# A decoder layer on one core: cross-attention heads on 64-row tiles, set-up spread over engines, new orders and banks, 71 expert blocks

## The chip, the core and the metric

The kernel runs on one core of one Trainium2 chip. Its engines are TensorE (PE in the profile, PEld its weight loads), VectorE (DVE), ScalarE (ACT), GpSimd (POOL) and SyncE (SP), each with its own queue of instructions; they wait for each other on semaphores. The metric is the time of one execution in microseconds (us), as the device measures it.

## The reference

128 sequences of 64 tokens with 128 features (8192 tokens) go through one decoder layer, all in float32:

```python
x = x + self_attention(layernorm(x))      # 16 heads of 8, rotary positions, causal softmax
x = x + xattn(layernorm(x), ctx)          # q, k, v from x and ctx; score = q k^T / dk, NO softmax;
                                          # (score v) wo + bo, residual, layer norm with gain and bias
x = x + ffn(layernorm(x))                 # 8 experts, top-1 by x @ centroids.T:
    # h = relu(xn @ w1[e].T + b1[e]); y = x + h @ w2[e].T + b2[e]; sigmoid(affinity) mixes y and x
```

As the cross-attention has no softmax, (q k^T) v is computed as q (k^T v), for each head a product of an 8x8 matrix.

## The kernel before

**Rounds.** The tokens are 64 tiles of 128, two a group, 32 groups. Each engine runs its own loop of 40 rounds (`rounds`); in round i it does each of its steps for group i minus that step's stage number (`stage(g, k, step)`), in a hand-searched order, the `one(g)` of its block. All waits are semaphore waits inside the steps. Buffers are double: `g - 2` must have been used before `g` is written.

**The way of a group.** VectorE `stats_x`, GpSimd `std_x`, ScalarE `norm_x`, TensorE `x_turned`, ScalarE `x_turned`; TensorE `queries_keys` (L560) and `values` (L568); VectorE `rotate` (L1104) and `partners` (the shuffle, L1114), GpSimd `rotated` (L1480), ScalarE `by_head` (L901). TensorE `max_scores` (L580, L588) gives scores in four banks; VectorE `row_max` (L1122, twice) reduces them, ScalarE `max_high` and GpSimd `max_low` (L1487) split the maxima in two bf16 parts, TensorE `max_rows` (L602) turns them, VectorE `max_by_head` (L1131) writes the shift. TensorE `scores` (L614, L622) writes shifted scores into the same four banks, ScalarE `exp` (L917, twice) empties them, TensorE `weighted` (L638, twice), VectorE `weighted_turned` and `inverse`, GpSimd `divide`, VectorE `turned_back`, TensorE `projected` (L655, L659), VectorE `x1_sum` (L1164, then statistics), GpSimd `std_x1`, ScalarE `norm_x1`, and so to the cross-attention: `ctx_turned`, `cross_keys_values` (L677, L681), `values_keys` (L702, k^T v on 32-column tiles of the array), VectorE `own_head` (L1174, keeps the heads' own 8x8 blocks), `cross_queries` (L689), `attended` (L717, on 32x32 tiles), `cross_output` (L723, L727), VectorE `y_sum`. Then `x2_sum`, `stats_x2`, TensorE `x2_turned` (L736) and `affinities` (L743), VectorE `choose`, TensorE `ranks`, VectorE `place` and `slots`, `alpha`, and GpSimd `scatter_rows` (L1570), two indirect DMAs that write 136 floats a token into its expert's part of `expert_rows` in DRAM. GpSimd also does `gain`, `offset_x1`, `std_y`, `std_x2`, `row_scalars` and `scaled_affinity`.

**Banks.** PSUM has eight banks; 0 to 3 are for `scores` and `max_scores`, 4 to 7 are shared by the other uses (`BANK`). `free` waits for the readers of a bank's former uses (`BEFORE`; in rounds 10 to 22 only for the first in the list).

**Set-up.** ScalarE issues four loads and then ten more (L1011, L1013). VectorE takes the mean out of the self-attention weights (L1093), then makes all masks, identities and picks (`masks_and_picks`, L1273 to L1310) after its round 0, and `bias_parts` (L1314 to L1348, biases split into three bf16 parts) after round 1. TensorE computes three constant products (L803 to L805).

**Late in the rounds.** From round 36 on, `expert_offsets` (L771) puts 16 products of single columns ahead of TensorE's round, four times. When the last counts are known, VectorE makes the block table, a chain of small operations (L1378 to L1398).

**Experts.** 72 blocks of 128 rows, each of one expert. SyncE loads a block's rows (L491), VectorE normalises (L1406), TensorE L819, L829, L840, ScalarE and VectorE the relu (L1040, L1416), GpSimd the base (L1612) and the index (L1615), VectorE the sum (L1424, L1429), GpSimd scatters 128 rows to the output (L1621).

## Time and profile before

| | us |
|---|---|
| median of the runs (lowest, highest) | 698.96 (697.45, 699.39) |
| the profiled execution | 700.01 |
| its span (first to last instruction) | 698.1 |
| TensorE busy | 595.6 (85%) |
| VectorE busy | 511.2 (73%) |
| GpSimd busy | 485.7 (70%) |
| ScalarE busy | 424.5 (61%) |

A row of a timeline gives start and length in us, engine, line and operation, what is written from what, shapes and a count; rows with the same line are merged if they follow each other. In brackets stands how long the engine was idle before it and what ended that ("remote": no event in the trace explains it; "issue": the engine waited for nothing that the profile shows). The ends of TensorE's products are modelled, so its completions are better read from who starts after them.

### The profile page before, as it was taken

Reading aid. Unit: us, or ns where it says so; the run is one execution under the profiler, and the core shown is the slowest. Engines: PE = TensorE matmul, PEld = TensorE weight load, DVE = VectorE, ACT = ScalarE, POOL = GpSimd, SP = SyncE. Lnnn points to the kernel's source line nnn. Section 1 sums busy time; section 2 is a strip of 40 time slices with the busy share of each in tenths; the row PEclk is TensorE's granted clock in tenths of the full one; section 3 lists DMA queues with packets and bytes.
Section 4 is the critical chain, followed back from the end, with each engine's and each line's share of the span. In section 5 each row is a group of like instructions: output and inputs, shape, how many; then the busy total and the mean of one; then the engine's idle time right before and its main releaser. Section 6 shows DMA issues by size and latency. Waiting matters only on the chain.

```text
span 698.1 us, 27653 instructions
## 1 busy us (share of the span) xinstructions
PE 595.6 (85%) x9104; PEld 453.4 (65%) x9136; DVE 511.2 (73%) x1813; ACT 424.5 (61%) x1154; POOL 485.7 (70%) x899
## 2 busy tenths in 40 slices
PE   3579888988888888888899888987858999999993
PEld 2246656666666566665666666655758989888893
DVE  5766887888788887888788887865455666666662
ACT  1347766767577666767677676764206666666661
POOL 2214676777767776777767776666644898898985
PEclk9999999999999999999999999999558999999997
DMA  4942111111111111111111111100022222222210
GB/s 125 168 137 85 49 38 37 34 40 49 42 33 40 49 33 41 34 40 49 37 37 41 42 40 34 33 23 18 9 61 53 60 61 62 61 64 56 65 51 5
DMA packets 53786, 35.61 MB, mean 51 GB/s; under 512 B 14464, under 2 KB 50049, under 8 KB 53648
## 3 DMA queue, kind: packets, MB, share of 16 engines
q1 hardware_dynamic: 47136, 23.29, 12.9%
q0 software_dynamic: 4352, 8.66, 3.7%
q10 hardware_dynamic: 2160, 1.87, 0.9%
q8 instruction: 79, 1.29, 0.8%
q14 instruction: 59, 0.48, 0.2%
HBM read 24.53 MB, written 9.80 MB: 49 GB/s over the span
## 4 chain that ended last, share of the span: by engine, by line
POOL 31%; DVE 22%; issue 21%; PE 18%; another core or an unknown queue 4%; POOLq 1%; DMA 1%; ACT 1%; DVEq 0%; SPq 0%; ACTq 0%
POOL bs L1612 8%; POOL qk L1480 5%; POOL pay L1542 4%; POOL rs_T L1507 3%; POOL out L1621 3%; DVE t__1 L1104 2%; PE side L659 2%; PE quad L622 2%; DVE shift L1131 2%; PE side L560 2%; DVE stat_T L1082 2%; POOL x L1516 2%; PE quad L614 2%; DVE x L1164 2%
## 5 line engine op out<-in xcount | busy, mean ns | idle before, releaser
L917 ACT ACTIVATE prob<-quad 128x1024 f32<-128x1024 f32 x64 | 65.8, 1032 | 85.9 <-remote 71.8
L1122 DVE TENSOR_REDUCE mx<-quad 128x16 f32<-128x1024 f32 x64 | 77.9, 1220 | 23.4 <-PE quad L588 23.4
L1621 POOL DMA_INDIRECT out<-yo,idi x72 | 77.9, 1081 | 21.1 <-issue 11.7
L901 ACT ACTIVATE ex<-qk,cf 128x512 f32<-128x512 f32 x128 | 81.8, 713 | 7.6 <-POOL qk L1480 7.6
L1570 POOL DMA_INDIRECT expert_rows<-pay,sli x64 | 67.4, 1053 | 21.3 <-issue 15.4
L840 PE MATMUL quad<-w,hT 128*128 x576 | 77.3, 277 | 1.0 <-DVE yb L1424 1.0
L840 PEld LDWEIGHTS quad<-w,hT 128*128 128x128 f32 x576 | 70.6, 193 | 1.8 <-issue 1.8
L1406 DVE TENSOR_SCALAR xh<-rb 128x128 f32<-128x128 f32 x72 | 47.6, 660 | 31.4 <-issue 26.5
L1612 POOL TENSOR_SCALAR bs<-rb 128x128 f32<-128x128 f32 x72 | 57.7, 802 | 10.7 <-DMA rb<-expert_rows 6.7
L1480 POOL TENSOR_TENSOR qk<-t__0 128x512 f32<-128x512 f32 x16 | 20.3, 1268 | 53.6 <-DVE t__0 L1114 48.3
L717 PE MATMUL side<-q,mt 32*32 32x64 f32 x1024 | 37.7, 225 | 19.3 <-issue 18.2
L1480 POOL TENSOR_TENSOR qk<-t__1 128x512 f32<-128x512 f32 x16 | 20.3, 1268 | 46.1 <-DVE t__1 L1114 46.1
L1051 ACT ACTIVATE w1b<-w,gb 128x512 f32 x72 | 51.7, 719 | 1.0 <-issue 1.0
L1164 DVE TENSOR_TENSOR x<-side,xr 128x256 f32<-128x256 f32 x32 | 13.6, 425 | 50.0 <-remote 33.6
L717 PEld LDWEIGHTS side<-q,mt 32*32 32x32 f32 x1024 | 24.0, 106 | 32.3 <-issue 28.6
L638 PE MATMUL side<-prob,vau 128*32 128x64 f32 x2048 | 42.4, 222 | 1.9 <-issue 0.6
L1429 DVE SCALAR_TENSOR_TENSOR yo<-yb,rb,bs 128x128 f32<-128x128 f32 x72 | 25.5, 355 | 25.2 <-DVE yb L1424 22.0
L560 PE MATMUL side<-xT,ws 128*128 128x256 f32 x128 | 38.5, 426 | 6.4 <-DVE t__0 L1104 5.9
L829 PE MATMUL quad<-xhT,w1b 128*128 128x128 f32 x288 | 41.4, 288 | 2.1 <-ACT w1b L1051 2.1
L829 PE MATMUL side<-xhT,w1b 128*128 128x128 f32 x288 | 41.3, 288 | 0.1
L1040 ACT ACTIVATE hT<-quad,b 128x128 f32<-128x128 f32 x72 | 22.6, 364 | 30.4 <-PE quad L829 22.0
L1040 ACT ACTIVATE hT<-side,b 128x128 f32<-128x128 f32 x72 | 22.5, 364 | 28.3 <-PE side L829 23.2
(195 smaller groups left out, 1708.6 us busy)
## 6 DMA issues: line engine op xcount, KB each, us to landing
rb<-expert_rows SPq DMA_DIRECT2D x72, 68.0 KB
xin<-in_x SPq DMA_DIRECT2D x32, 128.0 KB, 2.1
cin<-in_ctx SPq DMA_DIRECT2D x32, 128.0 KB, 2.2
xr<-in_x SPq DMA_DIRECT2D x32, 128.0 KB, 2.4
w<-in_w1t SPq DMA_DIRECT2D x4, 512.0 KB, 4.5
w<-in_w2t SPq DMA_DIRECT2D x4, 512.0 KB, 5.3
out<-yo,idi POOLq DMA_INDIRECT x72
expert_rows<-pay,sli POOLq DMA_INDIRECT x64
```

The costliest lines, as they stand in the source:

```text
L560: last = mm(BANK["queries_keys"][:, i * TG:(i + 1) * TG], w, xT[g.par][:, :], start=True, stop=True)
L717: last = mm(BANK["attended"][strip, own], mt2[g.par][strip, b, j, :], q2[g.par][strip, own], start=True, stop=True, tile_position=(32 * c, ...
L829: last = mm(HT[u][c // 2][:, (c % 2) * P:(c % 2 + 1) * P], w1b[u][:, c * P:(c + 1) * P], xhT[u][:, :], start=True, stop=True)
L840: last = mm(M[1][:, 0:D], hT[u][:, c, :], w2[:, bass.ds(e, 1), c, :], start=c == 0, stop=c == FC - 1)
L901: act(ex[g.par][:, i, :, :].rearrange("p a t -> p (a t)"), qk[g.par][:, :, :].rearrange("p a t -> p (a t)"), ACT.Copy, scale=own4[:, i:i + ...
L917: act(prob[g.par][:, 2 * h_:2 * h_ + 2, :], quad[:, 2 * h_:2 * h_ + 2, :], ACT.Exp).then_inc(*ac_a.done(f"e{h_}"))
L1051: act(w1b[u][:, :], w1[:, bass.ds(e, 1), :].rearrange("p e f -> p (e f)"), ACT.Copy, scale=gb[:, 0, bass.ds(e, 1)]).then_inc(*ffn["act_w1" ...
L1122: v.tensor_reduce(mx[g.par][:, 2 * h_:2 * h_ + 2, :], quad[:, 2 * h_:2 * h_ + 2, :].rearrange("p r (h k) -> p r h k", k=SQ), AX.X, ALU.max ...
L1480: v.tensor_tensor(qk[g.par][:, :, :], t1[g.par][:, :, :], t3[g.par][:, :, :], ALU.subtract).then_inc(*po_f.done("qk"))
L1570: v.indirect_dma_start(out=rows, out_offset=bass.IndirectOffsetOnAxis(ap=sli[g.par][:, j:j + 1], axis=0), in_=pay[g.par][:, j, :], in_offs ...
L1612: v.tensor_scalar(bs[q][:, :], rb[q][:, 0:D], rb[q][:, C_R:C_R + 1], rb[q][:, C_C:C_C + 1], ALU.mult, ALU.subtract).then_inc(*ffn["pool_ba ...
L1621: v.indirect_dma_start(out=o_rows, out_offset=bass.IndirectOffsetOnAxis(ap=idi[b.c % 4][:, 0:1], axis=0), in_=yo[b.c % 4][:, :], in_offset ...
```

## The change

- NBLK is 71: whatever the counts, 64 tiles in 8 experts fill at most 64 + 7 blocks.
- `values_keys` and `attended` use 64-row, 64-column tiles of the array (two strips for four); `mt2`, the mask and `own_head` are twice as wide.
- `ranks` does three products for four, with one more, zero, column group in `ohb`.
- Set-up: `masks_and_picks` and `bias_parts` are cut up. VectorE does `identities` (eight small operations) in round 0 before it centres the weights; `centred` (seven) and `picks` (twelve) behind `partners` of group 1; `key_value_bias` behind `max_by_head` of group 0 and `output_bias` behind that of group 1, eight operations each on 256 columns. ScalarE's `masks` (six copies: bvx, pick, two shifts, tri_b, negq_b) stands behind its `x_turned` of group 1; `max_scores` waits for it. TensorE's three constant products stand behind `queries_keys` of group 1, and write bank 4. GpSimd clears `pay` and `vau` behind `std_x` of group 1. The ten loads go from ScalarE's queue to SyncE's: three after round 0, seven after round 1. ScalarE issues `ws` first.
- The places of the uses in banks 4 to 7, the waits that go with them, and the orders of all five engines are new; stage numbers shift with them (TensorE's run from 1 to 7 for 0 to 6).

```diff
@@ constants of the program
-    NBLK = NT + E
+    NBLK = NT + E - 1
...
-        mt2 = two("mt2", [P, 2, J, 32])
+        mt2 = two("mt2", [P, 2, J, SQ])
...
@@ BANK (new places; scores and max_scores keep banks 0 to 3, queries_keys 7, cross_queries and values 6)
         BANK = {
+            "x2_turned": bank[4],
+            "cross_output": bank[6],
+            "x_turned": bank[7],
+            "weighted": bank[5],
+            "affinities": bank[4],
+            "x1_turned": bank[7],
+            "cross_keys_values": bank[6],
+            "max_rows": bank[4],
+            "ranks": bank[5],
+            "values_keys0": bank[4],
+            "values_keys1": bank[5],
+            "ctx_turned": bank[7],
+            "projected": bank[4],
+            "attended": bank[5],
...
-        N_CONST, N_LATE, N_WEIGHTS = 10, 4, 8
+        N_CONST, N_BIAS, N_LATE, N_WEIGHTS = 3, 7, 4, 8
         LOAD_AT = 4
+        KV_READY, OUT_READY = 8, 9
+        SETUP = bank[4]
...
             def late_loads(i):
 
+                if i == 0:
+                    for dst, src in ((cf[:, i1:cf.shape[1]], consts[:, i1:cf.shape[1]]), (nqf[:, :], negq),
+                                     (nkf[:, :], negk)):
+                        sp.dma_start(dst, src).then_inc(d_const, 16)
+                if i == 1:
+                    for dst, src in ((br[:, :, :].rearrange("p a d -> p (a d)"), brow.partition_broadcast(P)),
+                                     (wc[:, :, :], wcross), (cT[:, :], cent)):
+                        sp.dma_start(dst, src).then_inc(d_bias, 16)
+                    for q in range(4):
+                        sp.dma_start(wop[32 * q:32 * q + 32, :],
+                                     wself.rearrange("(r i d) a n -> i a r d n", r=4, i=4)[q, 5, :, :, :]
+                                     ).then_inc(d_bias, 16)
                 k = i - LOAD_AT
...
-                stage(g, 1, load_x)
-                stage(g, 3, load_ctx)
+                stage(g, 5, load_ctx)
                 stage(g, 5, load_again)
+                stage(g, 0, load_x)
...
@@ block.tensor: what a bank's use waits for (only the first of each list in the steady rounds)
+                "cross_output": [(ac_f, "V1", 3), (ac_t, "Q2", 0), (ac_t, "kv", 0), (dv_t, "y1", -1)],
+                "x1_turned": [(ac_f, "xT", 4), (ac_t, "cT", 1), (dv_f, "k2", 3), (ac_t, "xT", -1)],
+                "cross_keys_values": [(dv_t, "y1", -1), (ac_f, "V1", 2), (ac_t, "Q2", -1), (ac_t, "kv", -1)],
+                "max_rows": [(dv_r, "i1", -4), (ac_r, "xT", -4), (dv_t, "x1", -2), (dv_t, "mt", -3),
+                "values_keys0": [(dv_s, "x", 2), (dv_r, "i1", -2), (ac_r, "xT", -2), (dv_t, "x1", 0),
+                "values_keys1": [(dv_r, "tot", -2), (dv_a, "ot", 1), (ac_t, "A", -1), (dv_t, "mt", -1)],
+                "projected": [(dv_t, "mt", -1), (dv_s, "x", 1), (dv_r, "i1", -3), (ac_r, "xT", -3),
+                "attended": [(dv_t, "mt", 0), (dv_r, "tot", -2), (dv_a, "ot", 1), (ac_t, "A", -1)],
...
+            def constants():
+
+                pe.wait_ge(d_bias, 16 * N_BIAS)
+                pe.wait_ge(s_masks, 1)
+                to = SETUP
+                mm(to[:, 0:D], bvx[:, :], WO, start=True, stop=True)
+                mm(to[:, D:2 * D], mean_m[:, :], wc[:, 0, :], start=True, stop=True)
+                mm(to[:, 2 * D:2 * D + E], mean_m[:, :], cT[:, :], start=True, stop=True).then_inc(s_pe, 1)
+                setup["bank"] = to
...
-                    for c in range(4):
-                        strip = slice(32 * c, 32 * c + 32)
+                    for c in range(2):
+                        strip = slice(64 * c, 64 * c + 64)
                         for b in range(2):
                             rows_ = slice(64 * b, 64 * b + 64)
-                            last = mm(BANK[f"values_keys{b}"][strip, j * 32:(j + 1) * 32], kv2[g.par][rows_, j, 0, strip],
+                            last = mm(BANK[f"values_keys{b}"][strip, j * SQ:(j + 1) * SQ], kv2[g.par][rows_, j, 0, strip],
                                       kv2[g.par][rows_, j, 1, strip], start=True, stop=True,
-                                      tile_position=(64 * b, 32 * c))
+                                      tile_position=(64 * b, 64 * c))
...
-                        for c in range(4):
-                            strip = slice(32 * c, 32 * c + 32)
+                        for c in range(2):
+                            strip = slice(64 * c, 64 * c + 64)
                             last = mm(BANK["attended"][strip, own], mt2[g.par][strip, b, j, :], q2[g.par][strip, own],
-                                      start=True, stop=True, tile_position=(32 * c, 32 * c))
+                                      start=True, stop=True, tile_position=(64 * c, 64 * c))
                 last.then_inc(*pe_t.done("A"))
...
-                mm(bank_[:, 0:J * E], tri_b[:, :], ohb[g.par][:, :, :].rearrange("p j e -> p (j e)"),
+                mm(bank_[:, 0:(J + 1) * E], tri_b[:, :], ohb[g.par][:, :, :].rearrange("p j e -> p (j e)"),
                    start=True, stop=False)
-                for to, i in ((1, 0), (2, 0), (2, 1)):
-                    last = mm(bank_[:, to * E:(to + 1) * E], ones_b[:, :], ohb[g.par][:, i, :],
-                              start=False, stop=to == i + 1 == J)
+                mm(bank_[:, E:3 * E].rearrange("p (a e) -> p a e", e=E), ones_b[:, :],
+                   ohb[g.par][:, 0, :].unsqueeze(1).broadcast_to((P, 2, E)), start=False, stop=False)
+                last = mm(bank_[:, 2 * E:3 * E], ones_b[:, :], ohb[g.par][:, 1, :], start=False, stop=True)
...
@@ block.tensor, one round (old lines left out)
+                stage(g, 7, x2_turned)
+                stage(g, 6, cross_output)
+                stage(g, 1, x_turned)
+                stage(g, 4, weighted, 0)
+                stage(g, 7, affinities)
+                stage(g, 4, weighted, 1)
+                stage(g, 5, x1_turned)
+                stage(g, 5, cross_keys_values)
                 stage(g, 3, max_rows)
+                stage(g, 7, ranks)
                 stage(g, 1, queries_keys)
                 stage(g, 5, cross_queries)
                 stage(g, 3, scores)
+                stage(g, 5, values_keys)
+                stage(g, 3, ctx_turned)
+                stage(g, 2, values)
                 stage(g, 4, projected)
                 stage(g, 5, attended)
                 stage(g, 2, max_scores)
...
@@ block.scalar, one round (old lines left out)
+                stage(g, 8, token_ids)
                 stage(g, 4, max_high)
+                stage(g, 7, squares)
                 stage(g, 6, x1_turned)
                 stage(g, 8, exp_affinity)
+                stage(g, 6, cross_keys_values)
                 stage(g, 3, by_head)
                 stage(g, 6, cross_queries)
                 stage(g, 4, exp, 0)
+                stage(g, 4, exp, 1)
+                stage(g, 1, norm_x)
                 stage(g, 6, attended)
+                stage(g, 4, ctx_turned)
+                stage(g, 3, values)
                 stage(g, 7, x2_turned)
                 stage(g, 5, norm_x1)
                 stage(g, 1, x_turned)
...
@@ block.vector: where the pieces of set-up stand
+                    identities()
...
+                if g.n == 1:
+                    centred()
+                    picks()
...
+                if g.n == 0:
+                    key_value_bias()
+                if g.n == 1:
+                    output_bias()
...
-                                side[:, 2:2 + 2, 0:J * 32].rearrange("p b (j d) -> p b j d", d=32),
-                                headmask32[:, :].unsqueeze(1).unsqueeze(1).broadcast_to((P, 2, J, 32)), ALU.mult
+                                side[:, 0:0 + 2, 0:J * SQ].rearrange("p b (j d) -> p b j d", d=SQ),
+                                headmask64[:, :].unsqueeze(1).unsqueeze(1).broadcast_to((P, 2, J, SQ)), ALU.mult
...
@@ block.vector, one round (old lines left out)
+                stage(g, 8, x2_sum)
+                stage(g, 3, partners)
+                stage(g, 6, x1_sum)
+                stage(g, 8, stats_x2)
+                stage(g, 4, row_max, 0)
+                stage(g, 4, row_max, 1)
+                stage(g, 7, y_sum)
+                stage(g, 8, choose)
+                stage(g, 5, weighted_turned)
+                stage(g, 0, stats_x)
+                stage(g, 4, max_by_head)
                 stage(g, 5, inverse)
+                stage(g, 8, place)
+                stage(g, 2, rotate)
                 stage(g, 8, slots)
                 stage(g, 8, alpha)
                 stage(g, 5, turned_back)
+                stage(g, 6, own_head)
...
@@ block.gpsimd, one round (old lines left out)
                 stage(g, 7, std_y)
+                stage(g, 8, row_scalars)
                 stage(g, 5, divide)
                 stage(g, 1, std_x)
+                stage(g, 6, offset_x1)
                 stage(g, 8, scatter_rows)
+                stage(g, 5, std_x1)
                 stage(g, 2, rotated)
                 stage(g, 7, std_x2)
+                stage(g, 3, max_low)
+                stage(g, 7, scaled_affinity)
                 stage(g, 6, gain)
```

## Rows read from the trace of the kernel before

**Rows 1.** Windows: stretch; busy of PE, PEld, DVE, ACT, POOL; clock; DMA; GB/s.

```profile
0.00:22.00 22.00, 6.06 (x16) 3.71 (x16) 14.52 (x59) 3.62 (x8) 4.89 (x15) 1.00 0.65 127
...
145.00:431.00 286.00, 251.97 (x4880) 178.16 (x4898) 238.42 (x860) 198.81 (x540) 210.39 (x420) 1.00 0.13 40
```

**Rows 2.** Timeline of the set-up, all engines.

```profile
5.65 3.26 ACTq L1013 DMA_DIRECT2D wop<-in_wself  x4
...
7.25 0.55 DVE L1093 TENSOR_TENSOR ws<-ws,quad 128x384 f32<-128x384 f32 x1 [3.06 <-PE quad L505]
...
8.96 0.69 ACT L875 ACTIVATE xn<-xin,rs_L 128x128 f32<-128x128 f32 x2 [4.71 <-issue]
...
14.99 2.05 PE L560 MATMUL side<-xT,ws 128*128 128x256 f32 x4
...
21.59 1.66 DVE L1104 SCALAR_TENSOR_TENSOR t__0<-side,bc,cf 128x256 f32<-128x256 f32 x4
```

**Rows 3.** L614 and L1570 by source line: ns min/median/max, first and last start.

```profile
L614 PE MATMUL quad<-shift,pick x96: 379/379/634, 35.8 to 473.5; 128*128 128x512 bf16 x96
...
L1570 POOL DMA_INDIRECT expert_rows<-pay,sli x64: 957/1062/1202, 88.5 to 513.6; - x64
```

**Rows 4.** Timeline of TensorE in one even round.

```profile
302.95 1.12 PE L622 MATMUL quad<-ex,qk 32*64 32x256 f32 x32
...
304.13 0.61 PE L659 MATMUL side<-wop,ont 128*128 128x128 f32 x4
304.67 0.42 PE L717 MATMUL side<-q,mt 32*32 32x64 f32 x14
...
306.14 0.49 PE L717 MATMUL side<-q,mt 32*32 32x64 f32 x13 [0.44 <-issue]
...
309.40 0.60 PE L580 MATMUL quad<-negq_b,ii 64*128 64x512 bf16 x4
...
309.94 1.12 PE L588 MATMUL quad<-ex,qk 32*64 32x256 f32 x32
```

**Rows 5.** Timeline of GpSimd in the same round.

```profile
303.33 1.09 POOL L1570 DMA_INDIRECT expert_rows<-pay,sli  x1 [0.18 <-issue]
304.72 1.04 POOL L1570 DMA_INDIRECT expert_rows<-pay,sli  x1 [0.30 <-issue]
```

**Rows 6.** Timeline of ScalarE and VectorE in the same round.

```profile
304.32 0.61 DVE L1197 SCALAR_TENSOR_TENSOR pay<-yg,rs_U,x 128x128 f32<-128x128 f32 x2
...
306.26 1.02 ACT L917 ACTIVATE prob<-quad 128x1024 f32<-128x1024 f32 x1 [2.74 <-remote]
306.46 0.42 DVE L1164 TENSOR_TENSOR x<-side,xr 128x256 f32<-128x256 f32 x1 [1.53 <-remote]
...
307.55 0.74 DVE L1114 STREAM_SHUFFLE t__1<-t__1 128x512 f32<-128x512 f32 x1
...
308.17 0.48 DVE L1082 BATCH_NORM_STATS2 stat_R<-pay 128x6 f32<-128x128 f32 x2
```

**Rows 7.** Timelines of an early round, before the first scatter of rows.

```profile
64.25 1.02 ACT L917 ACTIVATE prob<-quad 128x1024 f32<-128x1024 f32 x1 [1.06 <-PE quad L622]
...
64.69 0.65 PE L717 MATMUL side<-q,mt 32*32 32x64 f32 x32
```

**Rows 8.** Groups by line, 145 to 431 us: busy us, mean ns | idle before, releaser.

```profile
L1174 DVE TENSOR_TENSOR mt<-side,headmask 128x128 f32<-128x128 f32 x20 | 5.6, 281 | 0.0
...
L602 PE MATMUL side<-ident_b,mt 128*32 128x64 bf16 x80 | 4.7, 194 | 17.6 <-POOL mt L1487 17.6
```

**Rows 9.** Chain of waits at the end of the rounds: start, us, what.

```profile
493.38 3.41 PE quad L771 x16
...
503.52 3.49 PE quad L771 x16
```

**Rows 10.** Timeline of GpSimd in the experts.

```profile
601.79 1.08 POOL L1621 DMA_INDIRECT out<-yo,idi  x1 [0.16 <-issue]
...
604.02 1.09 POOL L1621 DMA_INDIRECT out<-yo,idi  x1 [0.16 <-issue]
```

334 lines of the change are left out of this document (137 added, 197 removed).

## The prediction, made before the change was run

> **What bounds the kernel now.** I read the busy times by stage first, then the timeline of one round, then what its waits are. The span has three parts: a set-up, 32 groups moving through a pipeline that advances one group a round, and 72 blocks of the experts. In [rows 1] no engine is full in the rounds: from 145 to 431 us, TensorE is busy 252.0 of 286, VectorE 238.4, GpSimd 210.4, ScalarE 198.8. The first product of `scores` starts at 35.8 and the last group's at about 473 [rows 3]; with 31 steps between them that is 14.1 us a step, and the even rounds in the middle take 14.3 (286 us hold 20 of them). So a round is 14.3 us, against 11.9 of VectorE's work and 12.6 of TensorE's. The question is which loop of waits makes up the difference.
>
> The timeline of a round shows it. `scores` (L622) starts at 302.95 and its records end by 304.07; `projected` (L659) starts at 304.13 and lasts 0.61 [rows 4]. Yet ScalarE starts its exponential at 306.26 and VectorE starts `x1_sum` at 306.46, after 2.74 and 1.53 us of idling [rows 6]. In the same stretch the 32 products of `attended` (L717) come in three bursts, from 304.67 to 306.63, 1.96 us in all [rows 4]. In a round before any rows are scattered, the same 32 products take 0.65 us and the exponential starts at 64.25, right behind L622 [rows 7]. What is new in the later rounds is the pair of row scatters on GpSimd, at 303.33 and 304.72, ending at 305.76 [rows 5]. I read this as a **hold**: TensorE's completions are not reported from about 0.8 us after the first scatter's start until 0.4 us after the second one's end. That the scatter causes it is an inference from this coincidence. From `x1_sum` the loop runs on: the shuffle, then on GpSimd the rotated queries, two deviations, the gain, the offset, and only then the small sum for which `max_rows` (L602) waits, 17.6 us in 20 rounds [rows 8]; then shift, `scores`, `projected`, and again `x1_sum`.
>
> In the experts GpSimd sets the pace: a scatter starts at 601.79 and the next at 604.02, hence 2.23 us a block [rows 10].
>
> **The change part by part.**
>
> *One block fewer.* 71 for 72 takes out one beat of GpSimd, 2.2 us. The tables shrink by one column in 72: nothing.
>
> *Set-up.* Now VectorE has the centred weights at 7.80 (7.25 plus 0.55) but turns to the first `rotate` only at 21.59, with masks and bias parts in between; ScalarE issues its ten loads before its first norm at 8.96, and `queries_keys` starts at 14.99 [rows 2]. Afterwards only the small identities come first, and they lie in the wait for TensorE's mean product. ScalarE issues four loads, and SyncE ten others, seven of them queued ahead of its third load of x; the four of `wop` alone take 3.26 us to issue [rows 2], so that load goes out near 7.5 instead of at once after the first norm, and VectorE's third statistics, which stand ahead of the first `rotate`, end near 10.8. The chain is then: centred weights at 7.8, the transpose and copy of x about 0.8 more, the product 2.05 [rows 2], which ends near 10.7 as well. So `rotate` comes at about 10.8 instead of 21.59, 10.8 us earlier. What is late next: ScalarE's masks (some 3 us, ahead of the first `by_head`), TensorE's three constant products behind them, and VectorE's `centred` and `picks` ahead of the first row maxima. I let these take 1 us back. The two bias splittings (eight steps each) follow the first two shifts, where VectorE idled; if that cover were absent, each would cost about 3.3. Bounds: gain 3 (nearly all the moved work surfaces) to 12; I take 10, nearer the top, because VectorE was busy only 14.5 of the first 22 us [rows 1] and the early rounds are thin. `max_scores` waits on ScalarE's masks; behind it on TensorE stand round 3's products, which have nothing to do earlier.
>
> *Cross heads on 64-row tiles.* `values_keys` and `attended` go from 32 recorded products each to 16. The masked copy `own_head` doubles from 128x128 to 128x256: 281 ns now [rows 8]; the sum of 128x256 elements out of PSUM, `x1_sum`'s first step, takes 0.42 [rows 6]; so +0.14 us a round on VectorE. On TensorE, 32 products take 0.65 with about 0.21 for the last one alone: they follow each other by 14 ns, so halving their number saves at most 0.2, and their tiles are wider. I take 0, bounds -0.2 to +0.2. The Trainium skill ("TensorE: Matmul & The Clock Gate", section "Wait — 56ns, not 53.3ns?") says that start-to-start never drops below about 25 ns however small a product is. By that rule halving the products would save about 0.4 us in each of the two steps; the row with 14 ns speaks against it, and I leave it out.
>
> *Three rank products.* Four become three, 0.05 us at the most, off any wait: nothing.
>
> *Orders and banks.* Here lies the sum. Walk the new order with the old durations. VectorE's whole round, back to back, is 11.9 + 0.14 plus some 0.4 of small waits between dependent steps: 12.5. TensorE's floor is 14.3 less its wait at L602 (17.6/20 = 0.9) less 1.3 of hold in L717 (1.96 - 0.65): 12.1. GpSimd has 10.5 of work. A loop through both now decides: `projected` is put on the bank that `own_head` reads, and stands behind it. So per round: `own_head`'s end, a hop of 0.15, `projected` 0.65, `attended` 0.5, `max_scores` 0.55 + 1.12 + 0.15 until it is reported [rows 4], then VectorE from the row maxima to `own_head`. The last is 12.5 less what VectorE does outside the loop: `x2_sum` 0.61, shuffle 0.7, `x1_sum` 1.08 (306.46 to 307.54), the statistics of x2 0.6 (0.48 and their aggregates) [rows 6], together 3.0, so 9.5. Sum: 0.15 + 0.65 + 0.5 + 1.82 + 9.5 = 12.6, with hops **12.8 us a round without a hold**. `max_low` no longer stands behind the offset on GpSimd, and only three of its steps (two deviations, the rotation) lie ahead of it; it gets to it before the new place of `max_by_head`. The exponentials have `values_keys` to `attended`, about 2.4 us, to run beside; they need 2 x 1.02 [rows 6]. So I find no other loop over 12.6.
>
> Does the hold go? The scatter of a group now starts after `slots` and `alpha`, late in VectorE's round, with only `turned_back` and `own_head` behind them, which is while TensorE does `projected`, `attended` and `max_scores`. The first scatter's start to `projected`'s report was 303.33 to 306.3, 3.0 us [rows 5, 6]. If that stays, the loop is: `alpha`'s end, 0.15, 3.0, `x1_sum` 1.08, statistics 0.6, then the row maxima to `alpha` (9.5 less `turned_back` and `own_head`, 0.8: 8.7) = **13.5, with hops 13.6 us a round with the hold**. Bounds of this term: 12.6 to 14.3 and, if the hold adds to the first loop, above.
>
> About 27 rounds carry the full load (the first scatter at 88.5 us, the last `scores` at 473 [rows 3]). With the hold they gain 0.7 x 27 = 18.9; without, 1.5 x 27 = 40.5.
>
> *Drain.* The expert offsets (L771) stand ahead of the round on TensorE and are on the path: 3.41 and 3.49 us [rows 9], the second hiding some 2. TensorE's stages are one later, so three of the four parts come ahead of its last rank product instead of two. I count 1 us lost, bounds -2 to +4.
>
> *Sum*, against the profiled execution's 700.0 (median 699.0, so 1 less at the end): -2.2 - 10 + 1 - 18.9 = -30.1, hence 669.9 and **669 us**.
>
> **The rivals.**
> 1. *The hold goes away* (64-row tiles, half the products in flight, other neighbours). For it: no hold shows in the rounds without scatter, and none beside the experts' scatters, where TensorE works on whole tiles. Against: the scatters stay, and `max_scores` has the same 32x64 tiles as `scores`. 688.8 - 40.5 - 1 = 647.
> 2. *The order brings nothing*: another loop, or waits longer than my hops, keep 14.3; this is also the case that the search doesn't do what it says. For it: my walk counts hops of 0.15 us, and the banks are four for sixteen uses. Set-up and block alone: 688.
> 3. *Slower: the hold adds to the new loop.* The scatters now fall on `attended` and `max_scores`, whose report opens both row maxima; if max_scores is held the full 2.1 us (304.07 to 306.1) with nothing beside it, a round is 12.8 + 2.1 = 14.9, +16 us, and the total 704. It decides from the point where a round passes 14.7 (11.2 us gained elsewhere over 27 rounds is 0.41). Against: the scatter starts behind VectorE's last steps, and by then most of the wait lies beside `x2_sum` and the shuffle.
>
> **How the numbers follow.** Hold stays 0.47 (own range 660 to 680), rival 1 0.25 (640 to 656), rival 2 0.18 (682 to 692), rival 3 0.07, and 0.03 for a small net change. The range 643 to 689 leaves out the lower end of rival 1, the upper of rival 2 and rival 3. Two us (0.3%) are about what a measurement can tell from no change. Faster 0.91, same 0.02, slower 0.07.
>
> **What would show it.** Right: first `rotate` near 11 us and first `scores` near 26; steady rounds of 13.6; `x1_sum` or the first row maximum idle behind a late report while two scatters run; 71 blocks at 2.23. A round near 12.8 with the row maxima right behind L588 is rival 1; 14.3 with GpSimd or a bank wait ahead of `max_rows` is rival 2; L588's consumers 2 us late is rival 3. Wrong altogether if ScalarE's masks or the ten loads on SyncE's queue push the first rounds back, or if the drain grows by more than 4 us.

## The result, and the profile after

The changed kernel takes **682.8 us** (median, 682.6 to 683.3) against 698.6 us in the same comparison (697.5 to 699.4): a ratio of 0.978, interval 0.976 to 0.979. The forecast was 669 with a range of 643 to 689. Faster it is, but by 15.8 us and not by 30. The profiled execution took 682.6 us, with a span of 680.7, against 698.1 before, so 17.4 us of span are to be found. The ratios here and below are worked out over the single runs and are not those of two medians; they leave out one run of 896.8 us and one of 1295.9 us of the kernel before, in a slow state.

The windows answer to [rows 1]: stretch, its length, busy time of PE, PEld, DVE, ACT, POOL, clock, DMA share, GB/s.

```profile
0.00:22.00 22.00, 11.98 (x62) 6.58 (x62) 12.63 (x54) 10.15 (x23) 8.31 (x19) 1.00 0.42 109
145.00:431.00 286.00, 271.58 (x4409) 184.57 (x4436) 259.45 (x892) 214.15 (x564) 220.95 (x437) 1.00 0.14 40
```

TensorE does twice the work in the first 22 us (11.98 for 6.06), and in the rounds it goes from 252.0 to 271.6 busy us of 286. The timeline of the set-up, VectorE and then TensorE, answers to [rows 2]:

```profile
10.79 1.66 DVE L1223 SCALAR_TENSOR_TENSOR t__0<-side,bc,cf 128x256 f32<-128x256 f32 x4 [0.33 <-PE side L596]
...
25.65 0.29 PE L640 MATMUL side<-ident_b,mt 128*32 128x64 bf16 x4 [4.49 <-POOL mt L1536]
28.17 1.49 PE L653 MATMUL quad<-shift,pick 128*128 128x512 bf16 x3 [0.22 <-issue]
...
35.13 0.69 PE L686 MATMUL side<-cf,cin 128*128 128x128 f32 x2 [4.23 <-DMA cin<-in_ctx]
...
37.58 2.01 PE L626 MATMUL quad<-ex,qk 32*64 32x256 f32 x32
```

`rotate` starts at 10.79, 10.8 us earlier than before, and `max_rows` (L640) at 25.65, 7.7 earlier (before it was 33.3). Then TensorE stands 4.2 us for the first context, and the second `max_rows` comes at 42.8, where before had it at 46.7: the lead over the kernel before is down to 3.9.

One even round, from the timeline of all engines; it answers to [rows 4 to 6]:

```profile
306.13 0.61 PE L697 MATMUL side<-wop,ont 128*128 128x128 f32 x4
306.19 1.09 POOL L1619 DMA_INDIRECT expert_rows<-pay,sli  x1 [0.98 <-DVE pay L1349]
306.67 0.68 PE L755 MATMUL side<-q,mt 64*64 64x64 f32 x16
307.06 0.40 DVE L1290 TENSOR_TENSOR x<-side,xr 128x256 f32<-128x256 f32 x1
307.58 0.96 POOL L1619 DMA_INDIRECT expert_rows<-pay,sli  x1 [0.30 <-issue]
307.82 1.89 PE L626 MATMUL quad<-ex,qk 32*64 32x256 f32 x32
309.09 0.37 ACT L998 COPY av<-side 128x256 f32<-128x256 f32 x1 [1.72 <-remote]
...
309.77 2.36 DVE L1244 TENSOR_REDUCE mx<-quad 128x16 f32<-128x1024 f32 x2 [0.98 <-PE quad L626]
310.44 0.28 PE L761 MATMUL side<-bo,ones_b 128*128 128x256 bf16 x1 [0.36 <-ACT vau L934]
```

The **hold** is still there. `attended` (L755) ends at 307.35 by its record, yet ScalarE's copy starts at 309.09, and the 32 products of `max_scores` (L626) take 1.89 us instead of 1.12. But `projected` (L697), which ends 0.55 us after the first scatter's start, is reported on time: `x1_sum` (L1290) starts at 307.06. The round takes 13.72 us (`max_rows` at 149.8 and, 19 rounds on, at 410.5).

At the end of the rounds the chain of waits shows, against [rows 9]:

```profile
454.17 3.32 another core or an unknown queue
...
469.53 3.50 PE quad L809 x16
...
481.15 3.50 PE quad L809 x16
...
488.62 3.52 PE quad L809 x16
```

Three groups of offset products are on the path, and a held report of 3.3 us ahead of them. The chain before has two such groups and a piece of the same kind of 2.85 us:

```profile
474.52 2.85 another core or an unknown queue
```

The **drain**, from the last `max_rows` (451.0) to the first of the last group's two scatters (497.4), takes 46.4 us; before, 471.7 to 512.2, 40.5.

So the 17.4 us are: set-up and filling 4.5 (lead at the fifth `max_rows`, 81.1 against 85.6), rounds 16.2 (the lead is 20.7 at the last one), drain -5.9, experts 2.6 (183.3 us from that scatter to the end of the span against 185.9).

### The profile page after: what moved, and what is told of

It reads as the page before. It is cut to its first block, busy times and chain, and to the rows that moved or that the text cites. A ratio compares the mean times of both kernels' runs of the same rounds, so it can differ in the third digit from the quotient of the medians.

```text
span 680.7 us, 25449 instructions
## 1 busy us (share of the span) xinstructions
PE 601.9 (88%) x8031; PEld 448.2 (66%) x8063; DVE 522.9 (77%) x1804; ACT 432.8 (64%) x1156; POOL 486.3 (71%) x896
## 4 chain that ended last, share of the span: by engine, by line
PE 43%; issue 18%; POOL 12%; ACT 11%; another core or an unknown queue 7%; DVE 3%; DMA 2%; SPq 1%; POOLq 1%; ACTq 0%; DVEq 0%
POOL bs L1652 8%; PE quad L661 5%; PE side L677 5%; PE side L596 5%; PE side L719 4%; ACT prob L961 4%; PE quad L653 3%; POOL out L1661 3%; PE side L781 2%; ACT vau L934 2%; PE side L765 2%; ACT xn L917 2%; PE side L727 2%; PE side L707 2%
## 5 line engine op out<-in xcount | busy, mean ns | idle before, releaser
L1244 DVE TENSOR_REDUCE mx<-quad 128x16 f32<-128x1024 f32 x64 | 75.4, 1220 | 36.1 <-PE quad L626 36.1
L1619 POOL DMA_INDIRECT expert_rows<-pay,sli x64 | 65.8, 1029 | 41.7 <-DVE pay L1349 30.0
L961 ACT ACTIVATE prob<-quad 128x1024 f32<-128x1024 f32 x64 | 62.1, 1023 | 19.2 <-PE quad L661 19.2
L626 PE MATMUL quad<-ex,qk 32*64 32x256 f32 x1024 | 55.5, 407 | 1.7 <-issue 0.3
L1544 POOL TENSOR_TENSOR on<-ot,rd 128x128 f32<-128x128 f32 x64 | 25.2, 414 | 35.1 <-DVE rd L1274 35.1
L998 ACT COPY av<-side 128x256 f32<-128x256 f32 x32 | 11.9, 373 | 58.3 <-remote 44.9
L626 PEld LDWEIGHTS quad<-ex,qk 32*64 32x64 f32 x1024 | 26.7, 136 | 29.9 <-issue 28.2
L857 PEld LDWEIGHTS quad<-xhT,w1b 128*128 128x128 f32 x288 | 35.7, 195 | 5.0 <-issue 2.4
```

Source lines behind the costliest of these rows:

```text
L626: last = mm(quad[64 * b:64 * b + 64, r_, 256 * j:256 * j + 256], qk[g.par][strip, 0, own], ex[g.par][strip, :, 1, own], start=False, stop= ...
L857: last = mm(HT[u][c // 2][:, (c % 2) * P:(c % 2 + 1) * P], w1b[u][:, c * P:(c + 1) * P], xhT[u][:, :], start=True, stop=True)
L961: act(prob[g.par][:, 2 * h_:2 * h_ + 2, :], quad[:, 2 * h_:2 * h_ + 2, :], ACT.Exp).then_inc(*ac_a.done(f"e{h_}"))
L1244: v.tensor_reduce(mx[g.par][:, 2 * h_:2 * h_ + 2, :], quad[:, 2 * h_:2 * h_ + 2, :].rearrange("p r (h k) -> p r h k", k=SQ), AX.X, ALU.max ...
L1619: v.indirect_dma_start(out=rows, out_offset=bass.IndirectOffsetOnAxis(ap=sli[g.par][:, j:j + 1], axis=0), in_=pay[g.par][:, j, :], in_offs ...
```

## The experiments

The first four ran on a chip on which the kernel before took 658.5 us and not 698.6. That became the main finding. e3, e7 and e9 leave part of the computation out (most offset products; the routing of rows to their experts) and serve for their times alone. Each verdict below is a ratio to the kernel before on the same chip, and times in us are compared only between kernels on chips of one kind. The rounds are read off the timelines, from the starts of `max_rows` over 19 or 20 rounds in the middle.

| kernel | kernel before there, us | this, us | ratio (interval) | round, us | last `max_rows` to last scatter, us |
|---|---|---|---|---|---|
| before, profile shown | 698.6 | | | 14.32 | 40.5 |
| changed, profile shown | 698.6 | 682.8 | 0.978 (0.976 to 0.979) | 13.72 | 46.4 |
| e5 changed again | 696.1 | 678.7 | 0.976 (0.972 to 0.981) | 13.56 | 46.1 |
| e6 before again | 696.1 | 695.8 | | 14.23 | 39.9 |
| e7 plain stores | 696.1 | 803.7 | 1.156 (1.149 to 1.163) | 18.3 | |
| e8 load and offsets | 696.1 | 672.0 | 0.967 (0.960 to 0.975) | 13.66 | 40.7 |
| e12 and copy behind | 698.1 | 673.4 | 0.962 (0.959 to 0.964) | 13.68 | 41.6 |
| e1 context load back | 658.5 | 640.5 | 0.974 (0.971 to 0.978) | 12.50 | 42.4 |
| e2 scatters moved | 658.5 | 681.2 | 1.035 (1.033 to 1.038) | 13.57 | 49.7 |
| e3 no offset products | 658.5 | 640.9 | 0.973 (0.971 to 0.975) | 12.52 | 36.3 |
| e4 32-row tiles | 658.5 | 643.5 | 0.978 (0.975 to 0.981) | 12.46 | 42.6 |
| e9 stores, loads early | 658.8 | 644.1 | 0.977 (0.974 to 0.980) | 12.51 | |
| e10 as e12 | 658.8 | 639.1 | 0.970 (0.967 to 0.972) | 12.52 | 38.5 |
| e11 and 32-row tiles | 658.8 | 635.7 | 0.967 (0.965 to 0.970) | 12.45 | 35.5 |

**e1: the context load back to stage 3.**

```
-                stage(g, 5, load_ctx)
+                stage(g, 3, load_ctx)
```

> The context load goes back from stage 5 to stage 3 of SyncE's round, so that the first one is queued ahead of the masks and the expert weights, and all else is as in the changed kernel. Theory (the load is late and TensorE pays for it once): in the changed kernel TensorE stands 4.2 us at 35 us (the turning of the first context waits for its DMA), and the lead over the kernel before falls from 7.6 us at the first round of maxima to 3.9 us at the second. The wait goes, the lead stays near 7 us, and the time falls by 3.5 to 4.5 us, to 678 to 679.5. Rival (the stand-still is covered by something that is late anyway, or the early load delays the x loads or the masks): under 1.5 us of it stays, 681 or more.

TensorE's timeline, same place as above:

```profile
29.34 1.12 PE L661 MATMUL quad<-ex,qk 32*64 32x256 f32 x32
31.72 0.41 PE L686 MATMUL side<-cf,cin 128*128 128x128 f32 x2 [1.27 <-issue]
...
33.50 1.12 PE L626 MATMUL quad<-ex,qk 32*64 32x256 f32 x32
```

The wait for the load is gone (1.3 us of idling with no releaser stay), and more with it: L626 takes 1.12 us where it took 2.01 behind the stand-still. The granted clock was 1.00 over it, and 0.50 in the changed kernel (0.95 against 0.88 from 24 to 90 us). From the first to the second `max_rows` it is 12.0 us instead of 17.1, and nothing gives it back. In the time, against e4 on the same chip (the changed kernel itself did not run there), that is a ratio lower by 0.35% with intervals that overlap, 3.0 us of median and 3.9 of span; in the latter, e4's shorter rounds work against it. So the 5 us are shown by the trace, and the time bears out some 3 of them.

**e2: the scatters behind `gain` in GpSimd's round, some 10 us after their input instead of at once.**

```
-                stage(g, 8, scatter_rows)
                 stage(g, 5, std_x1)
...
                 stage(g, 6, gain)
+                stage(g, 8, scatter_rows)
```

> One step moved: GpSimd issues the two scatters of a round after the gain instead of before std_x1, some 8 us later, over TensorE's queue from the turned x2 to the cross keys instead of over projected, attended and the scores for the maxima. Theory A (a report of TensorE is held while a scatter is being issued, and only products on 32- or 64-row tiles are held): the last report of attended comes on time, ScalarE's copy of it no longer waits 1.7 us on an unknown queue, the scores for the maxima take 1.1 us again and not 1.9, the round goes from 13.7 to 12.8 to 13.2 us and the time to 662 to 670. Theory B (any report of TensorE is held by a scatter): the waits of 1.3 to 2 us appear behind whatever TensorE does beside the scatters (turned x2, cross output, weighted), the round stays within 13.4 to 14.0, the time within 675 to 690. Theory C (the hold belongs to the products in their place in TensorE's queue and not to the scatter): ScalarE still waits 1.7 us for attended, 680 to 685.

None of the three. On this chip nothing was held to begin with, as e1's round below shows, so that the run can't tell A from B or C, and it is slower by 3.5% than the kernel before. (Its round of 13.57 us and time of 681.2 lie within what B and C forecast; both were for the other kind of chip, and nothing is held here.) GpSimd's timeline says why:

```profile
297.32 1.11 POOL L1619 DMA_INDIRECT expert_rows<-pay,sli  x1 [0.17 <-issue]
298.73 0.95 POOL L1619 DMA_INDIRECT expert_rows<-pay,sli  x1 [0.30 <-issue]
...
301.05 0.77 POOL L1544 TENSOR_TENSOR on<-ot,rd 128x128 f32<-128x128 f32 x2
```

`divide` (L1544) now queues behind the scatters. Its input, the reciprocal, ends at 298.2; it starts 2.8 us later, and the turned-back rows, `own_head` and `projected` all wait for it. In e1 it starts 0.15 us after its input. That cost 1.1 us a round: moving one step past another is an experiment on the queue too. I had not looked at what would stand behind it.

**e3: the offset products left out but for one.**

```
-                for e in range(part * count, min(E, (part + 1) * count)):
-                    for c in range(FC):
+                if (part + 1) * count < E:
+                    return
+                for e in (E - 1,):
+                    for c in (FC - 1,):
```

> Part of the computation is left out: of the 64 products that fold the normalisation's offset into the experts' first bias (four groups of 16 in TensorE's queue in the last rounds, 3.5 us each) only the last one is issued. Theory (three of the four groups stand on the chain of the drain): from the last maxima to the last scatter 46.4 us become 36 to 41, and the time falls by 6 to 10 us, to 673 to 677. Rival (the groups stand in TensorE's idle time and something else made the drain 5.9 us longer than before): 0 to 2 us.

From the last `max_rows` to the last scatter: 36.3 us against 42.4 and 42.6 in e1 and e4, 6.2 less, as expected. In the time only some 3 us show (0.973 against 0.978 of e4), since in this trace the third `max_rows` came 15.1 us after the second instead of 12.7, with TensorE idle for nothing that the profile shows. The products are worth a little less than two of their four groups of 3.5 us. The 42.4 themselves are 4 less than in the profile shown; e1's chain has the same three groups and no held piece, so I put these 4 us down to the held reports.

**e4: the cross heads on 32-row tiles again.**

```
-                    for c in range(2):
-                        strip = slice(64 * c, 64 * c + 64)
+                    for c in range(4):
+                        strip = slice(32 * c, 32 * c + 32)
```

and the mask, the product under it and `attended` alike.

> One part undone: the cross heads' products (kv grams and attended) stand on 32-row tiles again, 32 products each instead of 16, with the narrower mask, and all else is as in the changed kernel. Forecast's term (the tiles are worth nothing but their dispatch, 16 products more of 14 ns, twice a round, less 0.14 us of VectorE): within 0.3 us a round, 680 to 690. Rival 1 (the 64-row tiles are what keeps the hold short, since fewer reports are outstanding): the round grows by 0.5 us or more, 695 and above. Rival 2 (the wider product of the own-head step costs VectorE more than TensorE wins): the time falls by over 1.5 us, under 681.

The groups by line between 145 and 400 us, of e1 (64 rows) and then of e4 (32 rows), busy us and mean ns:

```profile
L755 PE MATMUL side<-q,mt 64*64 64x64 f32 x320 | 13.6, 224 | 0.0
L1300 DVE TENSOR_TENSOR mt<-side,headmask 128x256 f32<-128x256 f32 x20 | 7.7, 383 | 0.1
```

```profile
L755 PE MATMUL side<-q,mt 32*32 32x64 f32 x672 | 13.6, 217 | 0.0
L1300 DVE TENSOR_TENSOR mt<-side,headmask 128x128 f32<-128x128 f32 x21 | 5.2, 248 | 0.1
```

For TensorE the tiles are a wash (0.68 and 0.65 us for all products of `attended` in the timelines); VectorE pays 0.135 us a round for the wider mask. The rounds are 0.04 us shorter with 32 rows. The time is the same as the changed kernel's by ratio, 0.978 both.

**e5 and e6: both kernels as they are.**

> The changed kernel as it is, for its trace beside those of the other experiments. The experiments so far ran on a chip on which the kernel before took 658.5 us instead of 698.6, and in their traces ScalarE's copy of attended follows its last product at once, with rounds of 12.4 to 12.5 us instead of 13.7. Theory A (the reports held beside the scatters belong to the chip or to its state at the time, not to the program): the rounds are either near 12.5 us without a wait of ScalarE on an unknown queue or near 13.7 us with 1.7 us of it, the same as in all kernels of this set that scatter, and the ratio to the kernel before is within 0.975 to 0.981 in both cases. Theory B (the moved context load or the 32-row tiles took the hold away): on a chip where the kernel before takes 658 us this one still has rounds of 13.5 us or more.

> The kernel before as it is, for its trace. Theory (the chip sets whether the reports are held, and the hold costs either kernel the same): where it takes about 658 us, its rounds take 12.9 to 13.2 us instead of 14.3, the scores for the maxima follow the scatter without a late report, and set-up, drain and experts differ by less than 2 us from the profile shown. Rival (the faster chip is faster everywhere): experts and drain are shorter by 5 % as well, and single instructions have shorter rows.

They landed on a chip like the first one. Theory A holds as far as it was tried: rounds of 13.56 us with the late reports, and a ratio of 0.976. Its other half, this kernel where nothing is held, never came up, nor did e6's theory, which was for such a chip. e6's rival, a chip that is faster everywhere, doesn't fit: from the last group's first scatter to the end it is 183.9 us in e5 and 183.0 to 183.1 in e1 and e4. The comparison that shows the hold is that of one piece of program on two chips. e1's round on the chip of 658.5 us, and e5's waits (us in all, times, longest) on the chip of 696.1, from 145 to 400 us:

```profile
281.40 1.09 POOL L1619 DMA_INDIRECT expert_rows<-pay,sli  x1 [0.97 <-DVE pay L1349]
281.89 0.68 PE L755 MATMUL side<-q,mt 64*64 64x64 f32 x16
282.68 0.37 ACT L998 COPY av<-side 128x256 f32<-128x256 f32 x1
282.80 0.95 POOL L1619 DMA_INDIRECT expert_rows<-pay,sli  x1 [0.30 <-issue]
283.04 1.12 PE L626 MATMUL quad<-ex,qk 32*64 32x256 f32 x32
284.36 2.35 DVE L1244 TENSOR_REDUCE mx<-quad 128x16 f32<-128x1024 f32 x2 [0.35 <-PE quad L626]
```

```profile
ACT av L998 <- remote: 27.5, 16, 1.9
```

The same instructions in the same order, scatters of the same 1.09 and 0.95 us, the first one 0.5 us ahead of `attended` in both (301.81 and 302.30 in e5). On the one chip the copy follows the last product by 0.1 us, in all 32 rounds; on the other it starts 1.6 to 1.8 us after it in most rounds. And e6 has the old kernel's hold again on that chip, as in [rows 6]:

```profile
304.30 1.02 ACT L917 ACTIVATE prob<-quad 128x1024 f32<-128x1024 f32 x1 [2.63 <-remote]
304.49 0.42 DVE L1164 TENSOR_TENSOR x<-side,xr 128x256 f32<-128x256 f32 x1 [1.44 <-remote]
```

Whether the reports are held is thus not in the program. The runs fell on four chips: two hold (e5 to e8; e12), as does the one of the profiles shown, and two don't (e1 to e4; e9 to e11). What in the chip does it stays open, and as each chip was visited once, it may be a state that it was in at the time. I have no trace of the kernel before on a chip without the hold; from its times alone, 695.8 less 658.5 over 27 rounds makes 1.4 us a round.

**e7 and e9: plain stores instead of scatters.**

```
-                    v.indirect_dma_start(
-                        out=rows, out_offset=bass.IndirectOffsetOnAxis(ap=sli[g.par][:, j:j + 1], axis=0),
-                        in_=pay[g.par][:, j, :], in_offset=None).then_inc(d_s[g.par], 16)
...
                 stage(g, 0, load_x)
+                stage(g, 8, store_rows)
...
+                    sp.dma_start(rows[bass.ds(g.n * TG + j * P, P), :], pay[g.par][:, j, :]
+                                 ).then_inc(d_s[g.par], 16)
```

> Part of the computation is changed: the routed rows are not scattered by GpSimd to their experts' places but stored in order by two plain transfers of SyncE's queue a round, and the expert stage reads them in that order; all other work and every wait is as in the changed kernel. Theory 1 (the scatters hold TensorE's reports, where they are held): on a chip whose rounds take 13.7 us they fall to 12.4 or less, and the time by over 25 us against the changed kernel. Theory 2 (GpSimd's queue is what 2.6 us of scatters cost, hold or not): on a chip without the hold the rounds fall from 12.5 to 12.0 or less. Theory 3 (neither): the rounds stay as in the changed kernel on the same chip, within 0.1 us.

e7 was far slower, 803.7 us, a ratio of 1.156 (1.149 to 1.163), on the chip that holds. Waits of its trace, and one round:

```profile
PE side L697 <- DMA cin<-in_ctx: 51.2, 14, 4.0
```

```profile
303.97 0.83 SPq L494 DMA_DIRECT2D expert_rows<-pay  x2
...
309.69 1.12 PE L766 MATMUL side<-q,mt 64*64 64x64 f32 x16
310.91 0.37 ACT L1009 COPY av<-side 128x256 f32<-128x256 f32 x1 [5.04 <-PE side L766]
```

The stores wait for a late step, and the loads wait behind them in SyncE's queue: rounds of 18 us, none of which says anything of a round's floor. But one thing can be read. Without GpSimd's scatters the copy follows `attended` by 0.1 us in all 32 rounds, on the chip where it takes 1.7 with them. So the scatters are needed for the hold, on the chips that have it; with rounds this different I call that strongly supported and not shown to the last.

> Part of the computation is changed as in e7: the routed rows are stored in order by SyncE's queue and not scattered by GpSimd. In e7 the stores held the context load behind them (TensorE waited 53 us for it in 14 of the profiled rounds), so the round says nothing of the scatters; here the context load stands at stage 3 besides, one round and more ahead of its reader. Theory 1 (GpSimd's scatters hold TensorE's reports on the chips where they are held): ScalarE's copy of attended starts 0.1 us after its last product in all rounds, and the rounds take 12.5 us or less on a chip whose scattering kernels take 13.6 to 13.7. Theory 2 (GpSimd's queue bounds the round of 12.5 us): on a chip without the hold the rounds fall under 12.2. Rival (the stores still hold the loads): TensorE waits for the context again, rounds over 13.7.

e9 landed on a chip without the hold. Its rounds take 12.51 us, just as with scatters (e1), while GpSimd is busy for 170 us of the 255 instead of 215:

```profile
145.00:400.00 255.00, 250.42 (x4314) 174.50 (x4310) 240.00 (x870) 203.01 (x548) 170.19 (x383) 1.00 0.16 45
```

So theory 2 falls: GpSimd's queue is no bound. TensorE is, with 250.4 us of 255, in e1 249.5. Theory 1's number could not be taken on this chip.

**e8: the load and another split of the offset products.**

```
-                count = -(-E // (TOTAL + 1 - NG - QUIET))
-                if part * count >= E:
+                split = (0, 0, 2, 6)
+                at = sum(split[:part])
+                if not split[part]:
                     return
...
-                for e in range(part * count, min(E, (part + 1) * count)):
+                for e in range(at, at + split[part]):
```

> Two parts together: the context load back at stage 3, and the 64 offset products split otherwise over the same four places of TensorE's queue (0, 0, 16 and 48 of them instead of 16 each), so that most stand behind the last ranks, where TensorE waits 7.8 us for the first expert block. Theory: the load gives 3.5 to 4.5 us as alone, the products 3.5 to 7 (two groups leave the chain of the drain; the last group of 10.5 us may end 1 to 3 us behind VectorE's table, which ends at 503.5 us in the changed kernel's trace); together 7 to 11 us under the changed kernel on the same chip, a ratio to the kernel before of 0.961 to 0.967. Rival (the drain's chain runs through VectorE and the held copies, not through the products): 4 us in all, 0.971 or more.

6.7 us less than e5 on the same chip (8.1 of span), 0.967 against 0.976, with intervals that overlap a little; expected were 7 to 11. The second `max_rows` follows the first by 12.0 us instead of 16.5, the drain is 5.4 us shorter, and one long piece of offset products is left in the chain; a held report is still there:

```profile
447.50 3.25 another core or an unknown queue
...
476.27 3.51 PE quad L810 x16
```

**e10, e12 (one kernel) and e11: ScalarE's copy of attended behind two others.**

```
-                stage(g, 6, attended)
                 stage(g, 4, ctx_turned)
                 stage(g, 3, values)
+                stage(g, 6, attended)
```

> The kernel of e8 with one line moved: in ScalarE's round the copy of attended stands behind those of the turned context and of the values instead of ahead of them. In the trace the copy waits 1.7 us for a held report, and the two others (0.38 and 0.76 us, inputs there since 306 us) queue behind it, until cross_output waits for the values' copy. Theory (that queueing is what the hold costs): where reports are held, the two copies go under the wait, the round falls from 13.7 by 0.8 to 1.2 us, the ratio to the kernel before from 0.967 to 0.925 to 0.94; where they are not held, the round stays within 0.1 us of 12.5 and the ratio within 0.003 of e8's kind, 0.962 to 0.967. Rival (the hold stops TensorE's own queue, the scores for the maxima take 1.9 us instead of 1.1 and the row maxima start at 309.8 all the same): less than 0.3 us a round, 0.960 or more in either state.

> The kernel of e10 once more, since e10 and e11 ran where no report is held, so that the moved copy had nothing to show. Worked out anew from the changed kernel's round at 306 us: TensorE's bias product of cross_output starts at 310.44, 0.36 us after the values' copy lets it; with that copy out of the way it could start once the turned x2 is done, near 309.97. Theory A (the loop runs through that copy): where reports are held, the round falls from 13.66 by 0.3 to 0.5 us, the time by 8 to 13 us, the ratio from e8's 0.967 to 0.949 to 0.956. Theory B (the scores for the maxima, 1.9 us instead of 1.1 beside the hold, and the row maxima at 309.8 set the loop): 13.6 us and more than 0.962 where reports are held. Where they are not held: rounds of 12.48 and 0.968 to 0.972 again, and the question stays open.

e10 ran where nothing is held and showed, as it had to, rounds of 12.5 us; its ratio, 0.970 (0.967 to 0.972), missed the 0.962 to 0.967 forecast. e12 ran on a holding chip. Its round, with L935 the values' copy, L999 the moved one and L1245 the row maxima:

```profile
302.46 1.09 POOL L1620 DMA_INDIRECT expert_rows<-pay,sli  x1 [0.97 <-DVE pay L1350]
302.95 0.68 PE L755 MATMUL side<-q,mt 64*64 64x64 f32 x16
303.79 0.76 ACT L935 COPY vau<-side 64x256 f32<-64x256 f32 x2
304.10 1.90 PE L626 MATMUL quad<-ex,qk 32*64 32x256 f32 x32
305.38 0.37 ACT L999 COPY av<-side 128x256 f32<-128x256 f32 x1 [0.82 <-remote]
306.07 2.36 DVE L1245 TENSOR_REDUCE mx<-quad 128x16 f32<-128x1024 f32 x2 [1.01 <-PE quad L626]
306.21 0.27 PE L761 MATMUL side<-bo,ones_b 128*128 128x256 bf16 x1
```

The copies went under the wait as meant, `cross_output` (L761) starts without a wait, and the round stays at 13.68: my theory of the copy falls, theory B holds for the round. What opens VectorE's part of it is the report of `max_scores`: from the first scatter's start (302.46) to the row maxima 3.6 us, and from the row maxima to the next round's scatter (316.1) 10.1 us.

e10 and e12 are one program on two chips, so their rounds can be laid side by side. In e10 the two parts are 2.95 and 9.53 us. So only 0.67 of the 1.2 us between the rounds is the late report. The other 0.53 is one small step of VectorE, the last of `choose`. Here it is in e12 and then in e10, with the multiplication of GpSimd's `gain` (L1580) next to it:

```profile
309.43 0.73 POOL L1580 TENSOR_TENSOR yg<-y,br 128x256 f32<-128x256 f32 x1
309.48 0.71 DVE L1343 SCALAR_TENSOR_TENSOR ohb<-ix,cf 128x16 bf16<-128x16 uint32 x1
```

```profile
290.80 0.17 DVE L1343 SCALAR_TENSOR_TENSOR ohb<-ix,cf 128x16 bf16<-128x16 uint32 x1
291.31 0.72 POOL L1580 TENSOR_TENSOR yg<-y,br 128x256 f32<-128x256 f32 x1
```

The late row maxima push VectorE's step beside GpSimd's multiplication, and there it takes until that one ends. In the one steady round of e12 in which it takes 0.17 us, the round is 13.15. The changed kernel has the same on the chips that hold (0.70 us in 18 of its 19 such steps from 145 to 400 us); no run moved either step away. The ratio, 0.962, lies between the two forecasts; with the rounds unchanged I can't say where the 0.5% against e8 come from, and e8's interval holds it.

> The kernel of e10 with the cross heads on 32-row tiles again. From e4 against e1 on one chip (rounds of 12.40 to 12.42 against 12.47 to 12.48): 0.05 to 0.08 us a round less, 1.5 to 2.5 us in all, if the difference is the tiles' (VectorE's own-head product is 128x128 instead of 128x256). Rival (the 16 further products of each stage are in flight when the reports are held and lengthen the hold): the same or up to 4 us more where reports are held.

3.4 us below e10 on the same chip, where 1.5 to 2.5 were expected; the two intervals overlap. The rounds are 0.05 to 0.07 us shorter, which makes 1 to 2 us, and the drain 3.0. The rival, a longer hold with more products in flight, could not be seen there.

## Why the prediction was off, by its own steps

**One block fewer.** 2.6 us for 2.2. GpSimd's beat is unchanged.

**Set-up: the step that failed on the queue.** The chain to the first `rotate` came out as worked out (10.8). The first `scores` start at 28.2 where I had 26, a lead of 7.6 us. What I left out was the other queue that the diff moves a load past. `load_ctx` went from stage 3 to stage 5 of SyncE, behind seven late loads; SyncE issues it at 27.5, where the kernel before did at 10.1, and it lands at 35.1. I had named masks and picks as what would be late next. It was the context, for 4.2 us, and another 0.9 behind it at a granted clock of 0.50 (e1). I took 10 us and 4.5 came. With that line back, the fifth `max_rows` stands at 75.3 in e8 against 85.0 in e6 on the same chip: 9.7.

**64-row tiles.** Forecast 0, with +0.14 us for VectorE; measured +0.135 there and about nothing in total (e4).

**Orders and banks, the large term.** Forecast 13.6 us with the hold and 12.8 without; measured 13.72 on the chips that hold and 12.5 on those that don't. The first number is right and the second 0.3 too high, and the way there was half wrong. I let `projected`'s report and `x1_sum` carry the hold; in fact `projected` slips out before it, and the row maxima behind `max_scores` carry it. That is rival 3's mechanism, with 0.67 us of lateness in place of its 2.1 and a round far below its 14.9. From the scatter to the row maxima my walk has 4.8 us and from there to the next scatter 8.7; measured are 3.6 and 10.1. One is 1.2 too long and the other 1.4 too short, 0.53 of that for VectorE's step beside GpSimd's `gain`, which I had at its short length (e12). That the sum came out at 13.6 is luck. Without the hold VectorE's loop isn't the last either: TensorE is full at 98%.

**Rival 1's premise** was that tiles or neighbours might remove the hold. They don't (e5), and the kernel before, with 32-row tiles, is held on the same chips (e6); e4 ran where nothing is held and says nothing of it. About its time of 647 appears on two chips all the same (643.5 in e4), for a cause that no rival of mine had: there the kernel before is faster by 37 to 40 us as well, and the ratio is nearly the same.

**Drain: the wrong size, and past its bound.** Forecast +1, within -2 to +4; measured +5.9. By my own list this is a sign of being wrong. The term was sized too small in its first part: the chain has three groups of offset products for two before, one more of 3.5 us, and e3 is 6.2 us shorter with 63 of the 64 products left out. I had not priced the hold in the drain either: the chain has a piece of 3.3 us behind a late report, where `own_head` waits for the gram with two scatters running, and where nothing is held the code of e1 drains in 42.4 us. But the chain before has such a piece too, 2.85 us, so by the chains the hold adds only about 0.5 to the difference. Some 2 of the 5.9 us stay open.

Sum: set-up +5.5, rounds +2.7, drain +4.9, block -0.4 is 12.7 us, which is the way from 669.9 to the profiled 682.6.

## To carry to other kernels

For each DMA in a diff, write down what it stands behind on its issuing queue after the change, and when its reader first needs it; here one such line was worth 5 us in the trace and about 3 in the time. Work that is put ahead of a pipeline's round at the end, as "quiet" filler, should go to the place where its engine waits for something that no reordering can shorten (here the first expert block, 7.8 us), and not be spread over the rounds. And before a wait is designed around, see whether it is on every chip: times and loop lengths don't carry over, and a ratio to the old kernel on the same chip does within a per cent (e10 and e12, one program, have 0.970 and 0.962, with intervals that don't touch). Two traces of one program, laid side by side step by step, show where the difference lies and what it drags along.

## What the runs showed of the hardware

- Beside GpSimd's row scatters TensorE's completions are seen 1.6 to 1.8 us late on some chips and 0.1 us late on two others, with the same program. With what follows from it, this costs 1.2 us a round (e10 and e12; an estimated 1.4 in the kernel before) and 35 to 40 us of either kernel (of the changed one by e4, which is the nearest to it without the hold). Projected's report, 0.55 us after the scatter's start, is not late; attended's, 1.2 us after it, is. In the same stretch 32 products with 26 of their weight loads done stand still for half a microsecond (L626: 1.89 us for 1.12).
- VectorE's last step of `choose` (128x16) takes 0.17 us, and 0.49 to 0.77 us beside GpSimd's `gain` (a multiplication of 128x256, 0.73 us) that began at about the same time or up to 0.27 us before it. There are 163 such long cases in the traces of all these kernels, and in every one the step ends 0.03 us behind that multiplication.
- Small products follow each other closer than 14 ns: 32 of them on 32-row tiles (`values_keys` in e4) take 0.48 us with 0.20 for a single one, hence 9 ns apart on the mean (most of their recorded starts are 7 ns apart). The Trainium skill ("TensorE: Matmul & The Clock Gate", section "Wait — 56ns, not 53.3ns?") has a floor of about 25 ns; the runs here don't agree with it for tiles that lie in different rows and columns of the array.
- In five of these kernels (e3, e9 to e12) the third `max_rows` comes 14.0 to 15.1 us after the second, in e1, e2, e4, e5, e7 and e8 12.7; the changed kernel has 13.9 in its first trace and 12.7 in e5. In the two whose chain I read there (e3, e10) TensorE stands 2.9 us ahead of the turning of a context, with no releaser that the profile shows; that context had landed long before (at 12.4 us in e10, for a product at 44.4). What it waited for is open.
